# Attention's latents stay on partitions: sums inverted by way of DRAM, scaled on VectorE, laid out by DMA

## What is computed

```python
scores = jnp.einsum('bhsd,bhtd->bhst', query, key) * scale
attn = jax.nn.softmax(scores.astype(jnp.float32), axis=-1).astype(query.dtype)
out = jnp.einsum('bhst,bhtd->bhsd', attn, v)
out = out.transpose(0, 2, 1, 3).reshape(B, S, H * VD)
return out @ o_w.T
...
x = x + ga * _L0_attn_ref(h, ...)
h = _layernorm(x, axis=-1) * (1 + cb) + sb
```

## Time and profile before

| | us |
|---|---|
| median of 3 runs | 2083.45 |
| the runs | 2078.28, 2083.45, 2084.25 |
| the profiled execution | 2077.61 |
| its span, first to last instruction | 2075.7 |
| busy: PE, DVE, ACT, POOL | 1918.5, 1354.4, 1389.4, 1347.8 |
| attention's copies of p_o, first and last start | 201.69, 1447.73 |

### The profile page before, as it was taken

One profiled execution on the slowest core, in us unless ns is written; L12 is line 12 of the kernel. 1 busy time (PEld: TensorE's weight loads), 2 busy tenths in 40 slices (PEclk: granted clock), 3 DMA queues, 4 the chain that ended last, 5 costly groups with the idle time before them and its releaser, 6 DMA issues. The chain is left out here.

```text
span 2075.7 us, 44742 instructions
## 1 busy us (share of the span) xinstructions
PE 1918.5 (92%) x14050; PEld 1015.4 (49%) x14050; DVE 1354.4 (65%) x2858; ACT 1389.4 (67%) x1924; POOL 1347.8 (65%) x804
## 2 busy tenths in 40 slices
PE   8969999999999999999999999998855499999996
PEld 6623444444444444444444444443733367777765
DVE  5867777777777877777777778771532245555553
ACT  5617888888888888888888888887520135555543
POOL 2327888888888888888888888888256313333330
PEclk9969999999999999999999999999977699999998
DMA  6179970000000000000000000000123429999988
GB/s 235 46 311 406 407 274 0 0 0 0 0 0 0 0 0 0 0 0 0 0 0 0 0 0 0 0 1 3 55 81 123 140 94 338 343 347 346 337 277 288
DMA packets 87873, 231.12 MB, mean 111 GB/s; under 512 B 12048, under 2 KB 45072, under 8 KB 87696
## 3 DMA queue, kind: packets, MB, share of 16 engines
q1 hardware_dynamic: 77072, 200.32, 27.0%
q0 software_dynamic: 10752, 30.16, 3.8%
HBM read 126.33 MB, written 104.10 MB: 111 GB/s over the span
## 5 line engine op out<-in xcount | busy, mean ns | idle before, releaser
L813 POOL TENSOR_TENSOR prob_lo<-prob,prob_hi 128x1024 f16<-128x1024 f32 x512 | 1085.1, 2141 | 246.8 <-ACT prob_hi L836 246.8
L885 DVE TENSOR_REDUCE maxes<-ring 128x1 f32<-128x512 f32 x1024 | 645.0, 683 | 195.4 <-PE ring L987 187.6
L834 ACT ACTIVATE prob<-p_s,prob_scale 128x1024 f32<-128x1024 f32 x512 | 570.3, 1114 | 262.1 <-PE p_s L1021 260.6
L836 ACT ACTIVATE prob_hi<-p_s,prob_scale 128x1024 f16<-128x1024 f32 x512 | 570.2, 1114 | 0.0
L987 PE MATMUL ring<-kr_hi,qr_hi 64*128 64x512 f16 x1024 | 379.6, 385 | 13.6 <-DVE qc_hi L872 7.4
L987 PE MATMUL ring<-kc_pair,qc_hi 64*128 64x512 f16 x1024 | 375.5, 384 | 0.0
L1289 POOL DMA_INDIRECT ranked_out<-y,dest x128 | 122.7, 959 | 268.6 <-DVE y L1591 265.4
L1021 PE MATMUL p_s<-qr_lo,kr_hi 64*128 64x512 f16 x1024 | 293.0, 377 | 0.0
L1021 PE MATMUL p_s<-qr_hi,kr_lo 64*128 64x512 f16 x1024 | 283.2, 377 | 0.0
L1021 PE MATMUL p_s<-qr_hi,kr_hi 64*128 64x512 f16 x1024 | 250.3, 382 | 1.6 <-ACT prob_hi L836 1.5
L1021 PE MATMUL p_s<-qc_lo,kc_one 33*128 33x512 f16 x1024 | 248.1, 379 | 0.0
(11 more groups left out here) (253 smaller groups left out, 2665.9 us busy)
## 6 DMA issues: line engine op xcount, KB each, us to landing
w<-in_experts SPq DMA_DIRECT2D x128, 608.0 KB
expert_rows<-zeros SPq DMA_DIRECT2D x129, 544.0 KB, 7.7
rows<-expert_rows SPq DMA_DIRECT2D x128, 136.0 KB
got<-ranked_out SPq DMA_DIRECT2D x16, 768.0 KB, 10.4
wqb<-in_wqb SPq DMA_DIRECT2D x8, 768.0 KB, 5.0
cbar<-in_woT SPq DMA_DIRECT2D x1, 2048.0 KB, 16.3
ranked_out<-y,dest POOLq DMA_INDIRECT x128
out<-x SPq DMA_DIRECT2D x16, 128.0 KB, 3.6
```

The costliest lines, as they stand in the source:

```text
L813: gp.tensor_tensor(prob_lo[s % NB][:, :], prob[s % 2][:, :], prob_hi[s % NB][:, :], ALU.subtract).then_inc(lo_ready, 1)
L834: act.activation(prob[s % 2][:, :], p_s[s % 2][:, :], ACT.Exp, bias=prob_scale[:, :], scale=SCALE / W_SCALE)
L836: act.activation(prob_hi[s % NB][:, :], p_s[s % 2][:, :], ACT.Exp, bias=prob_scale[:, :], scale=SCALE / W_SCALE).then_inc(p_ready, 1)
L885: v.tensor_reduce(maxes[:, at:at + 1], bank[:, :], AX.X, ALU.max).then_inc(ring_used, 1)
```

## The change

The turn and its two DVE steps are gone. p_o's copy goes to one of two att_t. SP sends the two rows of sums (512 values each, on one partition) to DRAM and fetches them back as 128 x 8; DVE inverts them at group 2 (`invert`); SP sends the reciprocals to DRAM and fetches each block's row back, broadcast to 32 partitions (recip_wide); DVE multiplies att_t by it, 96 partitions x 512 (`scale`), at the start of group 7; SP stores the two blocks into cbar, which now has 4 heads x 32 latents on partitions and tokens on columns, so `project` takes its stationary operand from cbar as it lies. turn_att and copy_turned are gone. A copy waits until the att_t it writes has been stored (freed). For the last half-head the same steps lie in `mixture`: invert after token tile 2, scale after tile 4, and product 8 waits for the store; the loads of the shared expert stand behind the broadcast. The ring keeps its length by a blank use, "pause", after the first maximum: PE and DVE count that maximum twice. The blanks are sent in fives, one batch per half-head, and SP's loop is written out. Two loads of the first stage share a semaphore, which PE awaits before two products instead of after them.

```diff
+        sums_dram = nc.dram_tensor("prob_sums", [2 * H, 2 * QC], F32, kind="Internal").ap()
+        recips_dram = nc.dram_tensor("prob_recips", [2 * H, 2 * QC], F32, kind="Internal").ap()
+        att_t = [sb(top, f"att_t{n}", QC) for n in range(2)]
+        recip_wide = [sb(top, f"recip_wide{n}", QC) for n in range(2)]
+        sums = sb(top, "sums", 8)
+        scaling = (att_t, recip_wide, sums, sums_dram, recips_dram)
+        moving = [top.enter_context(nc.semaphore(name)) for name in ("moved", "answered", "stored")]
...
+def send_sums(sp, k, scaling, done):
+    for c in range(2):
+        sp.dma_start(sums_dram[k:k + 1, c * QC:(c + 1) * QC],
+                     att_t[k % 2][c * CP + C:c * CP + C + 1, :]).then_inc(done, 16)
+def fetch_sums(sp, k, scaling, done):
+    sp.dma_start(sums[:, :], sums_dram[k:k + 1, :].rearrange("o (p j) -> (o p) j", p=P)).then_inc(done, 16)
+def send_recips(sp, k, scaling, done):
+    sp.dma_start(recips_dram[k:k + 1, :].rearrange("o (p j) -> (o p) j", p=P), sums[:, :]).then_inc(done, 16)
+def spread_recips(sp, k, scaling, done):
+    for c in range(2):
+        sp.dma_start(recip_wide[k % 2][c * CP:c * CP + C, :],
+                     recips_dram[k:k + 1, c * QC:(c + 1) * QC].to_broadcast([C, QC])).then_inc(done, 16)
+def store_heads(sp, k, scaling, cbar, done):
+    h, half = k // 2, k % 2
+    for c in range(2):
+        at = h // 4 * S + half * 2 * QC + c * QC
+        sp.dma_start(cbar[h % 4 * C:(h % 4 + 1) * C, at:at + QC],
+                     att_t[k % 2][c * CP:c * CP + C, :]).then_inc(done, 16)
...
+        BLANKS = E * S // (4 * P) + 1
         EVENTS = [what if c is None else (c, n) for g in range(len(MAX_AT)) for now in plan(g) for what, c, n, part in now
                   if c is None or (what == "max" and part == 1)]
         MAXIMA = [(c, n) for g in range(len(MAX_AT)) for now in plan(g) for what, c, n, part in now if what == "max" and part == 1]
+        EVENTS.insert(1, "pause")
         USES = len(EVENTS)
+        assert USES % RING == 0
+        def uses_of(what, first):
+            return 2 if what == EVENTS[0] and not first else 1
         def use_of(m, what, first=False, more=True, after=True):
             place = EVENTS.index(what)
...
             sp.wait_ge(zero_rows, 3)
-            with sp.Fori(0, E * S // (4 * P) + 1) as n:
-                sp.dma_start(rows[ds(n, 1), :, :].rearrange("a p n -> (a p) n"), zeros[:, :]).then_inc(zeroed, 16)
-            gate, lower, limits, numbers, tokens, own, regions = routing
...
-            sp.wait_ge(zeroed, 16 * (E * S // (4 * P) + 1 + DK + 6))
+            def clear(first, last):
+                for n in range(first, last):
+                    sp.dma_start(rows[n, :, :], zeros[:, :]).then_inc(zeroed, 16)
+            for k in range(2 * H - 1):
+                sp.wait_ge(o_copied, k + 2)
+                send_sums(sp, k, scaling, moved)
+                sp.wait_ge(moved, MOVES * k + 32)
+                fetch_sums(sp, k, scaling, moved)
+                if k:
+                    sp.wait_ge(stored, 32 * k)
+                    sp.sem_inc(freed, 1)
+                sp.wait_ge(answered, 2 * k + 1)
+                send_recips(sp, k, scaling, moved)
+                sp.wait_ge(moved, MOVES * k + 64)
+                spread_recips(sp, k, scaling, moved)
+                clear(min(5 * k, BLANKS), min(5 * k + 5, BLANKS))
+                sp.wait_ge(answered, 2 * k + 2)
+                store_heads(sp, k, scaling, cbar, stored)
+            sp.wait_ge(stored, 32 * (2 * H - 1))
+            sp.wait_ge(zeroed, 16 * (BLANKS + DK + 6))
...
+                v.tensor_reduce(maxes[:, at:at + 1], bank[:, :], AX.X, ALU.max).then_inc(ring_used, uses)
...
-            def copy_out(m):
+            def copy_out(m, half):
                 v.wait_ge(o_mm, 16 * m + 16 + NB)
-                v.tensor_copy(att_t[:, :], p_o[:, :]).then_inc(o_copied, 1)
-            def turn(half, h, use, bank):
-                v.wait_ge(ring_mm, use + 1)
-                src = bank[:, :].rearrange("p (b s n) -> p b s n", b=4, s=2)
-                r = recip[:, :].rearrange("p (b s n) -> p b s n", b=4, s=2)
-                step(v.reciprocal(r, src[:, :, :, C:C + 1]))
-                dst = cbar[:, half * 8 * HC:(half + 1) * 8 * HC].rearrange("p (s b n) -> p b s n", s=2, b=4)
-                v.tensor_tensor(dst[:, :, :, ds(h * C, C)], src[:, :, :, 0:C], r.to_broadcast([P, 4, 2, C]),
-                                ALU.mult).then_inc(ring_used, 1)
-                v.wait_ge(ring_used, use + 1 + RING)
+                v.wait_ge(freed, m + 1)
+                v.tensor_copy(att_t[half][:, :], p_o[:, :]).then_inc(o_copied, 1)
+            def invert(m):
+                v.wait_ge(moved, MOVES * m + 48)
+                v.reciprocal(sums[:, :], sums[:, :]).then_inc(answered, 1)
+            def scale(m, half):
+                v.wait_ge(moved, MOVES * m + MOVES)
+                v.wait_ge(o_copied, m + 2)
+                v.tensor_tensor(att_t[half][0:CP + C, :], att_t[half][0:CP + C, :], recip_wide[half][0:CP + C, :],
+                                ALU.mult).then_inc(answered, 1)
...
+                    copy_out(m - 1, 1 - half)
                 for g in range(len(MAX_AT)):
-                    for now in plan(g, first, more, after):
+                    if g == 2 and not first:
+                        invert(m - 1)
+                    if g == len(MAX_AT) - 1 and not first:
+                        scale(m - 1, 1 - half)
+                    for now in plan(g, more, after):
...
+                    last.then_inc(ring_mm, uses)
...
-            def turn(m, use, bank):
-                pe.wait_ge(o_copied, m + 2)
-                pe.wait_ge(ring_used, use + 1)
-                for b in range(4):
-                    last = pe.transpose(bank[:, b * P:(b + 1) * P], att_t[:, b * P:(b + 1) * P], ident[:, :])
                 last.then_inc(ring_mm, 1)
...
+            spread_recips(sp, last, scaling, moved)
             for n in range(2):
                 sp.dma_start(ws[n][:, :], a["experts"][E + n, :, :]).then_inc(ld_ws, 16)
+            sp.wait_ge(answered, 2 * last + 2)
+            store_heads(sp, last, scaling, cbar, stored)
...
-            def copy_turned(t):
-                act.wait_ge(ct_mm, t + 1)
-                if t >= 2:
-                    act.wait_ge(att_mm, t - 1)
-                act.copy(ctb[t % 2][:, :], p_ct[t % 2][:, :]).then_inc(ct_ready, 1)
...
+            def invert():
+                v.wait_ge(moved, MOVES * (2 * H - 1) + 48)
+                v.reciprocal(scaling[2][:, :], scaling[2][:, :]).then_inc(answered, 1)
+            def scale():
+                att_t, recip_wide = scaling[0][1], scaling[1][1]
+                v.wait_ge(moved, MOVES * 2 * H)
+                v.tensor_tensor(att_t[0:CP + C, :], att_t[0:CP + C, :], recip_wide[0:CP + C, :], ALU.mult).then_inc(answered, 1)
...
+                if t == 2:
+                    invert()
+                if t == 4:
+                    scale()
...
-            def turn_att(t):
-                if t >= 2:
-                    pe.wait_ge(ct_ready, t - 1)
-                for g in range(4):
-                    last = pe.transpose(p_ct[t % 2][:, g * P:(g + 1) * P],
-                                        cbar[:, t * HC + g * P:t * HC + (g + 1) * P], ident[:, :])
-                last.then_inc(ct_mm, 1)
             def project(t):
-                pe.wait_ge(ct_ready, t + 1)
+                if t == T // 2:
+                    pe.wait_ge(stored, 64 * H)
+                if t == 0:
+                    pe.wait_ge(col_ready, 1)
                 if t >= 2:
                     pe.wait_ge(x_used, t - 1)
                 for g in range(4):
-                    last = pe.matmul(p_y[t % 2][:, 0:D], ctb[t % 2][:, g * P:(g + 1) * P], wov[:, g * D:(g + 1) * D],
+                    last = pe.matmul(p_y[t % 2][:, 0:D], cbar[:, g * S + t * P:g * S + (t + 1) * P], wov[:, g * D:(g + 1) * D],
                                      start=(g == 0), stop=(g == 3))
```

More of the change, by code:

```diff
@@ L58 @@
 BATCH = 2
+MOVES = 96
 class Chain:
@@ L742, in attention, with plan @@
         BEGUN = [[sum(len(MAX_AT[i][c]) for i in range(g)) for c in range(2)] for g in range(len(MAX_AT))]
-        def plan(g, first=False, more=True, after=True):
+        def plan(g, more=True, after=True):
             rounds, at, done, open_max = [], [0, 0], list(BEGUN[g]), [False, False]
@@ L748, in plan @@
                 now = []
-                aside = {(1, 0): ("turn", not first), (6, 8): ("rows", more)}.get((g, len(rounds)))
-                if aside and aside[1]:
-                    now.append((aside[0], None, None, None))
+                if (g, len(rounds)) == (6, 8) and more:
+                    now.append(("rows", None, None, None))
                 for c in range(2):
@@ L779, in use_of @@
                 place -= 1
-            if not more:
-                place = -2
             return USES + USES * m + place, ring[place % RING]
```

(33 more changed lines are left out.)

54 lines of the change are left out of this document (27 added, 27 removed).

## The result

The changed kernel takes 2147.7 us (median of four, 2145.2 to 2148.1) where the kernel before takes 2082.8 (four, 2078.3 to 2084.3): ratio 1.0313, 95% interval 1.0295 to 1.0331. It is slower by 65 us; I had said 2116, slower by 33. The profiled execution has a span of 2145.9 us against 2075.7, so 70.2 us are to be found.

What follows compares the result with a forecast made beforehand. PE was taken to bound attention: 2077.6 - 18.3 + 63.5 - 1.9 - 7.6 = 2113.3 us, raised to 2116 by half the profiled run's difference from the median; range 2092 to 2150 us, meant to hold 80%.

Steps and rivals of the forecast that it cites:

- The bound, and what goes: Attention loop: PE is busy throughout; dropping 31 turns of 0.59 us saves 18.3 us.
- scale is held by POOL: DVE before group 0: scale waits out POOL's step, delaying PE 2.33 or 2.04 us in 29 half-heads, 63.5 us.
- The ring's blank use: Group 0: the third maximum, no longer the fourth, waits for the first's reading; PE wants it 1.31 us in.
- rival (c): Attention loop: PE's granted clock falls after each wait, losing 3.4 us 29 times, 99 us, total 2212; chance 7%.
- The stage behind: Attention's tail and token tiles: dropped transposes save 1.9 and 7.6 us, the latter with zero as other bound.
- The trips: Sums and reciprocals through DRAM: sums take 7.0 us, at worst 8.8; cost zero, bounds 0 to 1 us a half-head.
- rival (b): Trips come late at invert, beyond 9.5 us of room; 1 us late costs 29 us, total 2142; chance 8%.
- three signs that I had named for a wrong prediction: scale lasts 0.7 us, invert shows a wait on a DMA, or the loop's granted clock is under 1.

Runs made afterwards that it cites:

- scale_group5: Changed kernel with scale moved ahead of group 5's maxima and the blank use behind group 1's first maximum; ratio 0.9909 to the kernel before.
- one_input: Changed kernel with scale made a tensor_scalar by 1.0, one SBUF input instead of two, same place; ratio 1.0258 to the kernel before.
- pause_late: Changed kernel with the ring's blank use behind the last maximum instead of the first; ratio 1.0364 to the kernel before.

## Why the prediction was right and wrong

**The bound, and what goes.** Right. PE was the bound, and scale_group5, in which nothing new stands in its way, gives 14.6 of the 18.3 us for the turns; 2.6 of the rest (29 x 0.09) are PE's longer wait for DVE in group 0, which this step of the sum had left out.

**scale is held by POOL.** Right in place, size and consequence: 2.04 to 2.12 us where I had about 2.2, the wait at the third maximum, and a group of 6.00 us where I had 6.09. Undisturbed half-heads take 41.89 and 41.97 us; by my terms they would be 40.23 + 2.33 - 0.59 = 41.97 and 40.60 + 2.04 - 0.59 = 42.05, each 0.08 too long. Too narrow was the reason: it isn't the second SBUF input alone (one_input).

**The ring's blank use.** Right for its own 0.22 us (0.22 measured), of little weight beside the hold.

**PE's clock.** This is the step that failed: the sum has no term for it. I held rival (c) apart with 7%, since the fall that I had read in the trace of before came after 4.28 us of idling, and a wait of 2.5 us was shorter. The waits are 2.3 us, and 17 of the 29 are followed by a fall. The same trace had a warning that I didn't read. At the end of its attention PE idles three times, for 1.48, 1.25 and 0.86 us (it is busy for 6.56 of the 10.5 us up to 1448.5), and then the granted clock is 0.50. PE in order of time, then the stretch behind:

```profile
1444.70 0.41 PE L1034 MATMUL p_o<-prob_hi,c_hi 128*64 128x512 f16 x2 [1.48 <-POOL prob_lo L813]
1446.78 0.41 PE L1034 MATMUL p_o<-prob_hi,c_hi 128*64 128x512 f16 x2 [1.25 <-POOL prob_lo L813]
```

```profile
1448.50:1455.30 6.80, 5.55 (x20) 4.57 (x21) 0.79 (x3) 1.17 (x2) 1.71 (x9) 0.50 0.44 152
```

So 4.28 us was no bound to reason from. Of the rival's price of 99 us the number of falls was too high (17, not 29), and so was the loss in each (1.64 us: 3.4 us at half the clock, not 6.8). A term of 28.6 us was missing from the sum, and a rival that had all of it or nothing could not supply it. What decides which of the waits brings a fall stays open: one_input has 12 falls with waits of about 2.0 us, pause_late 18 with waits of 1.9 and 0.2.

**The stage behind.** Mis-sized: 5.8 us instead of 9.5. PE's work there fell by 7.5 us, but its idle time grew by 1.7. In the four traces taken beside the kernel before at 2077.3 us the stretch is 6.3 to 9.3 us shorter than before. The 2.2 us more from there to the end (557.0 against 554.8) are within what these traces differ by, 552.5 to 557.9.

**The trips.** Right that they cost nothing, wrong in the length of the first: 3.1 us, not 7.0. The trip of the reciprocals takes 3.8. The nearest landings, of table loads and of rows of 128 KB, were a poor measure for a few KB, and rival (b) deserved less than its 8%.

**Together:** 2113.3 by my sum, 28.6 for the clock and 3.7 for the stage behind make 2145.6, against 2147.8 for the profiled execution. The 2.2 left are attention's later start (1.2) and the rest of the program (2.2), less the 1.2 that my terms had too much in attention. That the range of 2092 to 2150 held is luck: it had been drawn wide for the trips, which had no part in it, and the clock used up the room. Two of the three signs that I had named for a wrong prediction came true: the loop's granted clock is under 1, and invert waits on a DMA, though only in the last half-head, where DVE has no maxima to read.

## What to carry to other kernels

Where an engine that sets the pace gets a new wait, price the wait and then ask what its clock does afterwards: here a wait of 2.3 us on TensorE cost 1.64 us more in 17 of 29 cases, and a wait of 0.9 us nothing more. Put a VectorE step that GpSimd can hold (here tensor_tensor and tensor_scalar within SBUF, not tensor_reduce) where both VectorE and GpSimd have time: in the wrong place it stands still until GpSimd's running step is over, in the next best it delays GpSimd, and only the slack of what waits for either tells which place is free. A blank slot in a ring belongs where nobody is late.
